# A graph network's sort and message passes: ScalarE's function set loaded before each layer, VectorE's mask operations one turn later, and a shorter empty burst on TensorE in three chunks of four

## The reference, cut

```python
def L0(x, src, dst, edge_attr_32):            # 5 layers
    for l in range(5):
        h = leaky(x @ W1[l] + b1[l]) @ W2[l] + b2[l]              # per node
        e = leaky(edge_attr @ We1[l] + be1[l]) @ We2[l] + be2[l]  # per edge
        msg = h[src] * e * dot_scale[l]
        agg = segment_sum(msg, dst, num_segments=3125)
        out = x + agg * res_w[l]
        x = layernorm(out) * ln_g[l] + ln_b[l]
    return x
x = layernorm(x + L0(x, ...))
x = layernorm(x + L1(x, ...))    # plain graph convolution
x = layernorm(x + L2(x, ...))    # two attention convolutions, softmax over the edges of each dst
x = layernorm(x + L3(x, ...))    # relu(x[src] + edge_attr_64), summed by dst
```

## Time and profile before

| | us |
|---|---|
| median of 3 runs (9173.51 to 9197.65) | 9191.92 |
| profiled execution, own time | 9174.3 |
| its span | 9172.8 |

### The profile page before, as it was taken

How to read it: one execution, slowest core, us unless ns; L and a number is a source line. 1 busy time by engine, 2 the same in 40 slices (tenths; PEclk the granted TensorE clock), 3 DMA queues, 4 the chain that set the end, 5 groups by cost and what they waited for, 6 DMA issues and landing times. The chain is left out here.

```text
span 9172.8 us, 305358 instructions
## 1 busy us (share of the span) xinstructions
PE 6676.0 (73%) x86569; PEld 5135.1 (56%) x86577; DVE 5985.6 (65%) x18295; ACT 3335.7 (36%) x5533; POOL 3246.3 (35%) x5198
## 2 busy tenths in 40 slices
PE   5899999344435766666667667666688899899887
PEld 4566665233324655555556456555566577677666
DVE  7445544799996766666666667566677555455677
ACT  2444444122223333433433433333344233233343
POOL 3666666444422443443444344344200000000254
PEclk9888988655556777777777677777799899899999
DMA  3666666233344775675677576577544111111487
GB/s 97 168 172 176 180 174 173 65 82 82 83 152 121 192 190 163 188 190 164 173 198 203 141 197 184 159 190 191 147 147 144 61 64 65 45 65 64 118 229 203
DMA packets 1790244, 1330.15 MB, mean 145 GB/s; under 512 B 1259701, under 2 KB 1482604, under 8 KB 1780410
## 3 DMA queue, kind: packets, MB, share of 16 engines
q1 hardware_dynamic: 1149466, 924.40, 33.4%
q0 software_dynamic: 261536, 328.49, 14.1%
q10 hardware_dynamic: 379008, 74.48, 4.6%
HBM read 1034.27 MB, written 291.36 MB: 145 GB/s over the span
## 5 line engine op out<-in xcount | busy, mean ns | idle before, releaser
L521 POOL DMA_DIRECT2D big<-rows x3384 | 1842.4, 545 | 4218.5 <-issue 2393.9
L1277 PE MATMUL ps<-big 128*128 128x64 bf16 x31584 | 2017.0, 209 | 1152.9 <-DVE big L1737 716.6
L1277 PEld LDWEIGHTS ps<-big 128*128 128x128 bf16 x31584 | 1586.9, 104 | 1556.5 <-issue 1287.3
L1266 PE MATMUL ps<-big 128*128 128x64 bf16 x31584 | 1346.0, 206 | 119.5 <-DVE big L1701 51.4
L1266 PEld LDWEIGHTS ps<-big 128*128 128x128 fp8e4 x31584 | 1213.2, 106 | 239.9 <-issue 165.9
L1013 ACT CAST big<-big 128x512 bf16<-128x512 f32 x1128 | 697.0, 618 | 1728.6 <-DVE big L1714 1408.0
L783 POOL DMA_INDIRECT rows<-big x800 | 980.5, 1226 | 688.2 <-issue 344.7
L1714 DVE TENSOR_TENSOR big<-ps,big 128x512 f32<-128x512 f32 x940 | 648.9, 690 | 582.4 <-DMA big<-rows 316.8
L1019 ACT CAST big<-big 128x512 bf16<-128x512 f32 x1316 | 813.0, 618 | 582.7 <-issue 431.1
L1737 DVE TENSOR_TENSOR big<-big 128x512 bf16<-128x512 f32 x1316 | 902.7, 686 | 4.2 <-ACT big L1019 3.5
L1502 DVE SCALAR_TENSOR_TENSOR big<-big 128x1000 f32<-128x1000 f32 (+1 forms) x300 | 359.3, 1198 | 700.3 <-ACT big L905 700.1
(11 more groups left out here) (256 smaller groups left out, 8880.5 us busy)
## 6 DMA issues: line engine op xcount, KB each, us to landing
big<-ohdD SPq DMA_DIRECT2D x658, 512.0 KB, 4.3
big<-ohsD SPq DMA_DIRECT2D x658, 256.0 KB, 2.8
big<-rows POOLq DMA_DIRECT2D x3384, 32.0 KB, 3.4
big<-rows SPq DMA_DIRECT2D x3384, 32.0 KB, 3.4
big<-maskD SPq DMA_DIRECT2D x50, 1600.0 KB, 6.6
big<-rows ACTq DMA_DIRECT2D x2256, 32.0 KB, 3.3
big<-keyT SPq DMA_DIRECT2D x100, 488.3 KB
ohdD<-big SPq DMA_DIRECT2D x188, 256.0 KB, 2.5
```

Of the source, the lines that this page charges most:

```text
L521: eng.dma_start(edge[:, s.r, j, :], rows[bass.ds(v[s.r * (hi - lo) + j - lo], P), col]).then_inc(landed[s.r], 16)
L1266: last = pe.matmul(pG[g.r][:, j * D:(j + 1) * D], ohsR[:, g.r, j * P:(j + 1) * P].bitcast(F8), slices[:, g.r, q // QUAD, c * D:(c + 1) * D ...
L1277: last = pe.matmul(pacc[:, bass.ds(w[j], D)], hot[:, g.r, j * P:(j + 1) * P], parts[:, g.r, c, j * D:(j + 1) * D], start=False, stop=False ...
```

## The change

Three edits.

1. `act.preload_act_table(ACT.Ln)` before each layer's `edge_pass`: ScalarE loads the function set of the logarithm there, and the compiler finds it in place in the loops behind.
2. `steps` takes a number `late`. VectorE calls it with 1: three turns unrolled ahead instead of two, and its mask work in turns 3 to 42 instead of 2 to 41. ScalarE, POOL and SP keep their turns.
3. The twelve empty matmuls stay only in chunks with j = 0; in chunks with j = 1, 2 and 3 there are two.

```diff
-        def steps(eng, body, aside=None):
+        def steps(eng, body, aside=None, late=0):
 
-            for i in range(2 * U):
+            for i in range((2 + late) * U):
                 body(Step(i // U, i % U))
-            cuts = [2] + ([2 + (k + 1) * UNITS for k in range(MASKS)] if aside else []) + [TRIPS]
+            cuts = [2 + late] + ([2 + late + (k + 1) * UNITS for k in range(MASKS)] if aside else []) + [TRIPS]
...
                 act.wait_ge(w_free, l + 1)
                 hold(act)
+                act.preload_act_table(ACT.Ln)
                 edge_pass(l * NG, False, bass.ds(l * D + D, D), log_counts)
...
-                    for _ in range(12 if m == 0 else 0):
+                    for _ in range(0 if m else 12 if j == 0 else 2):
                         pe.matmul(bank(4), zerob[:, :], each(iota1b[:, :], 4), start=True, stop=True)
...
-                steps(dve, body, fix_counts)
+                steps(dve, body, fix_counts, 1)
```

## The result

The changed kernel takes 9228.74 us (median of six runs, 9199.07 to 9253.56), the kernel before 9173.09 us beside it (six runs, 9170.93 to 9197.65). The ratio is 1.0053, 95% interval 1.0029 to 1.0077: **slower by 0.5%**, where 1.2% faster was forecast. The time lies inside the range that was given, 8980 to 9250, and on the other side of no change from the forecast, 9080. The executions of the changed kernel spread over 54 us, twice those of before.

What follows compares the result with a forecast made beforehand. It took TensorE's clock and SP's key loop (14.2 us a chunk) to bound the sort, VectorE's mask waits the layers. 9174 - 150 + 40 = 9064, on the median's scale 9082, forecast 9080 us; range 8980 to 9250.

Steps and rivals of the forecast that it cites:

- +40 us: Sort: cutting empty matmuls in three of four chunks loses time to the clock; bounds -120 and +335 us.
- 11.2 + 3 + 0.4 + 5.5: Sort: us for a short chunk run low to the end: warm time, low first part, stretched empty matmuls, low 128-row part.
- One that does not goes by the floor, 14.2: Sort: a short chunk not beginning at the low clock takes 14.2 us, set by SP's key-loading loop.
- half of the short ones each: Sort: half the short chunks begin at the low clock and take 17.4 us, half take 14.2 us.
- TensorE will wait about 3 us in it for keys, where the clock is lost today: Sort: a warm short chunk of 11.2 us waits about 3 us for keys, and the clock falls there.
- -150 us: Layers of L0: preload and late masks together, nine tenths of 168 us; between -60 and -168 us.
- L1774 then finds its Ln made a turn ago: Layers, VectorE's masks one turn later: the remaining 112 us of waiting for ScalarE's logarithm goes, as upper bound.
- For the first message there is room: Layers: TensorE's and the DMAs' results for the first message behind the masks are there before the masks end.
- rival 3: Layers: the masks' wait moves to edges or TensorE, only the table loads' part is won; -20 us, 9172 us, chance 0.10.
- -56 us: Layers, ScalarE's preload: VectorE waits 11.2 us a layer less for the logarithm once its table loads are gone.
- the price of nothing: Layers: forty table loads before the cast cost nothing today, and the new load a layer was taken as 0.
- Rival 1: Sort: only the long burst brings the clock back; +206 us there, 9248 us with -150 in the layers, chance 0.21.

Runs made afterwards that it cites:

- the run with keys first: Kernel before with SP loading a chunk's keys ahead of the wait for scattered rows, and bursts of 12, 2, 2, 2: 9222.63 us, ratio 1.0071.
- ScalarE's loads first: Kernel before plus preload and late masks, with ScalarE issuing its two edge loads before the cast of the message two groups back: 9031.79 us, ratio 0.9851.

## Why the prediction was wrong

**The sort, and the direction.** The term was +40 us, measured +113 alone and +131 in the profile. The prices were right: a short chunk at full clock was put at 11.2 us and measured 11.36, one wholly low at 11.2 + 3 + 0.4 + 5.5 = 20.1 and measured 19.81. That the clock can come back outside a burst was right as well, 15 of 34 rises. Three slips in the working are small: 15.7 us a chunk over 15.42 is 0.3 x 99 = 30 us and not 40, the loop of the earlier trace rows gives 42.4 / 3 = 14.1 and not 14.2, and the 64-row rows give a ratio of 1.85 and not 1.9. Two steps failed.
- "One that does not goes by the floor, 14.2" and "half of the short ones each". The keys' loop is no floor for a chunk that follows slow ones: keys are ahead then, and the 16 chunks at full clock took 11.36, not 14.2. That the loop would bound a long row of chunks at full clock is not shown by any run; there never was one.
- "TensorE will wait about 3 us in it for keys, where the clock is lost today." The clock was lost with no key late, in the work between two short bursts: 19.8 us of waits in the changed kernel, none in the run with keys first, and the clock low for 64% and 54% of the sort. Every rise lay in a burst before, and every wait for keys of 1.6 us or more came with a fall, and I made the wait the only cause of a fall. The trace of before spoke against it already: of its 36 falls up to 1600 us 17 have no wait for keys in the 14 us before them. What a burst did for a chunk that had the clock already, I never asked. As a result the short chunks took 16.6 us on average instead of 15.8, the long ones 16.95 instead of 15.5.

**The layers.** The term was -150 us; measured -69 in the profile, -84 and -87 where the layers' edits stood alone. Here too two steps failed.
- "L1774 then finds its Ln made a turn ago. What remains of the 168.5 us, 168.5 - 56 = 112 us, goes." Idle time carries the name of what came last. Under ScalarE's logarithm lay VectorE's own L1772, 0.31 us a time, 200 times, 62 us, which stayed (61.9 in the profile after, 61.8 with ScalarE's loads first). Only 168.5 - 62 = 106 us were to be had.
- "For the first message there is room." The timeline ended with that message. The third one of the turn, six microseconds further on, already waited for edge rows in the kernel before:

```profile
3795.88 0.69 DVE L1714 TENSOR_TENSOR big<-ps,big 128x512 f32<-128x512 f32 x1 [1.51 <-DMA big<-rows]
```

  and in the changed kernel it waits longer:

```profile
3896.23 0.69 DVE L1715 TENSOR_TENSOR big<-ps,big 128x512 f32<-128x512 f32 x1 [1.84 <-DMA big<-rows]
```

  That is rival 3, with its place, and it got a chance of 0.10 because I spoke against it with the wrong message. In the later mask chunks the quarter of a microsecond that L1775 gave (4.5 / 8 - 0.31) became a longer wait here: from one message of r = 0 to the next, the second chunk, third with fourth, and fifth averaged 14.76, 15.12 and 14.42 us a turn before, and 14.65, 15.07 and 14.52 after. What was won, 8 turns a layer at 1.7 us or 68 us in all, was won in the first mask chunk.

**The preload.** The term, -56 us, was right alone (-57), from the right rows, and so was the price of nothing for the loads ahead of the cast and for the new one. The Trainium skill (ScalarE: Activation LUTs, What ACT_TABLE_LOAD costs) has 2.66 us for a switch, of which 1.38 are a drain. The forty on the path gave back 57 us, 1.4 us each, and the trace of before shows no drain of that length: in each of the forty the engine is idle for 0.02 us or less on either side of the load. One of them on ScalarE's timeline:

```profile
3645.21 0.62 ACT L1019 CAST big<-big 128x512 bf16<-128x512 f32 x1 [0.54 <-DVE big L1731]
3645.84 1.28 ACT L1052 ACT_TABLE_LOAD   x1
3647.14 0.63 ACT L1052 ACTIVATE big<-big,tiny  x1
```

What I didn't see is that late masks make this edit redundant.

**Rival 1** gave 9248 us, 19 above the result, and those 19 us are the median of before, which is 9173 in six runs and was 9192 in three. That its change of +56 us is the measured one is luck: the sum, +206 and -150, is made of two errors that cancel, 17.5 us a chunk where 16.67 were measured, and the same -150. Rivals 1 and 3 were both partly true, in different stages. I had given each of them only beside the forecast's value for the other stage. Worked out together, +113 and -87, they leave "slower" well within reach, and a chance of 0.21 for it was too low.

## What to carry to other kernels

A wait in the profile is named for what came last; before it is counted as a gain, look at what came second, in the same place (here the engine's own last result) and in the rest of the period (here a DMA two messages on), over one whole period and not up to the first instruction that looks free. A burst of empty work that brings the clock back may also be what keeps it: count the falls, and ask what each chunk would run at without its burst, before taking it out of the chunks that seem not to need it. And what an order by hand puts behind a late wait, such as SP's keys behind the scatters, is often cheaper to move than any work is to remove: it gave 114 us here, and no other single edit gave more.

## What the hardware showed that I had not expected

- ScalarE's queue issues DMAs while its table load runs: 0.23 us after the load of 1.28 us began. The load held up the engine's cast (it starts at 3654.88, 0.02 us behind the load's end), and not its DMA issues.
- TensorE stayed at the low clock for at least 94% of a stretch in which it was busy for 1790 of 1821 us (no burst at all), with matmuls of 32, 64 and 128 rows and short waits; and 18 empty matmuls in four chunks held the clock better as 12, 2, 2, 2 than as 5, 4, 5, 4 (16.4 to 16.7 against 17.6 us a chunk, the latter in one run).
- The part of a chunk with the 128-row matmuls does not always bring the clock back: 21 chunks ran through its 10.8 us (960.45 to 971.20) without a rise.
